# First experts' up products in three half-precision products, and the second attention's turned maxima one slot later

## The reference, cut to what matters

```
# layer 0, mixture of 8 experts (2048 tokens, capacity 256 each)
logits = xt @ Wg;  probs = softmax(logits)
sel    = top 256 tokens of each expert by probs     # which token goes where
out    = sum_e gate[:, e] * (gelu(xt @ W1[e]) @ W2[e])   # W1[e] 128x256, W2[e] 256x128
# layer 1, cross attention: 16 heads of 64, keys of valid length only
scores = rope(q) @ rope(k).T / 8, masked;  attn = softmax(scores);  out = attn @ v
```

## Time and profile before

| | |
|---|---|
| median of 3 runs | 2943.0 us (2940.43 to 2944.17) |
| the profiled execution | 2939.36 us |
| its span | 2937.2 us |
| TensorE busy | 2638.0 us (90%) |
| VectorE busy | 2006.5 us (68%) |
| ScalarE busy | 1450.8 us (49%) |
| GpSimd busy | 1374.3 us (47%) |
| first experts | 862 to 993.4 us of the span |
| second attention, its iterations | about 1047 to 2690 us |

### The profile page before, as it was taken

One profiled execution on the slowest core, in us unless ns is written; L12 is line 12 of the kernel. 1 busy time (PEld: TensorE's weight loads), 2 busy tenths in 40 slices (PEclk: granted clock), 3 DMA queues, 4 the chain that ended last, 5 costly groups with the idle time before them and its releaser, 6 DMA issues. The chain is left out here.

```text
span 2937.2 us, 82056 instructions
## 1 busy us (share of the span) xinstructions
PE 2638.0 (90%) x32600; PEld 1569.0 (53%) x32600; DVE 2006.5 (68%) x6348; ACT 1450.8 (49%) x2243; POOL 1374.3 (47%) x1221
## 2 busy tenths in 40 slices
PE   3679999999989569999999999999999999996598
PEld 2423333333355536666666666666666666664365
DVE  3468888888856567667766766766667667662655
ACT  2247777777744035546446455455464454443222
POOL 2000000000000038877878878878778788785100
PEclk8789999999989779999999999999999999998799
DMA  5421111111010110000000000000000000001000
GB/s 156 144 89 24 24 27 22 25 22 25 21 30 1 64 37 7 19 13 7 18 13 7 17 13 7 26 5 19 13 8 18 13 7 7 7 2 51 0 0 15
DMA packets 109630, 75.20 MB, mean 26 GB/s; under 512 B 43907, under 2 KB 101579, under 8 KB 108752
## 3 DMA queue, kind: packets, MB, share of 16 engines
q1 hardware_dynamic: 109264, 70.08, 8.5%
HBM read 56.61 MB, written 13.43 MB: 24 GB/s over the span
## 5 line engine op out<-in xcount | busy, mean ns | idle before, releaser
L1485 ACT ACTIVATE a_probs<-psS 128x1024 f32<-128x1024 f32 (+1 forms) x448 | 431.7, 964 | 630.0 <-PE psS L1366 625.9
L645 ACT ACTIVATE a_probs<-psS 128x1024 f32<-128x1024 f32 (+2 forms) x512 | 443.5, 866 | 207.0 <-PE psS L586 206.6
L1802 POOL TENSOR_TENSOR a_acc<-a_acc,a_probs 128x512 f32<-128x512 f32 x320 | 407.3, 1273 | 225.1 <-ACT a_probs L1485 221.9
L1389 PE MATMUL psX<-a_probs,a_values 128*64 128x256 f32 x3328 | 445.6, 385 | 1.6
L672 DVE CUSTOM_DVE_ANT_0 a_junk<-psT,a_mask 128x384 f16<-128x384 f32 (+1 forms) x683 | 378.2, 573 | 61.3 <-PE psT L562 41.6
L1804 POOL TENSOR_TENSOR a_acc<-a_acc,a_probs 128x512 f32<-128x512 f32 x320 | 407.1, 1272 | 25.1
L1646 DVE CUSTOM_DVE_ANT_0 a_junk<-psT,a_mask 128x400 f16<-128x400 f32 (+1 forms) x514 | 282.6, 573 | 153.8 <-PE psS L1341 86.3
L1646 DVE CUSTOM_DVE_ANT_0 a_junk<-psS,a_mask 128x400 f16<-128x400 f32 (+1 forms) x510 | 280.7, 573 | 150.9 <-PE psT L1341 88.3
L974 POOL MEMSET r_ones<- 128x128 f16 x1 | 0.2, 205 | 694.4 <-POOLq L719 694.4
L1389 PEld LDWEIGHTS psX<-a_probs,a_values 128*64 128x64 f32 x3328 | 224.1, 137 | 105.2 <-issue 24.6
L1776 POOL TENSOR_TENSOR a_klo<-a_kt,a_khi 128x400 f16<-128x400 f32 (+1 forms) x256 | 242.7, 948 | 18.6 <-ACT a_khi L1537 18.6
(11 more groups left out here) (332 smaller groups left out, 5561.4 us busy)
## 6 DMA issues: line engine op xcount, KB each, us to landing
a_kd<-p_kst SPq DMA_DIRECT2D x24, 416.0 KB, 3.4
a_wq<-in_wq SPq DMA_DIRECT2D x64, 128.0 KB, 2.1
a_keys<-a_kd SPq DMA_DIRECT2D x96, 75.0 KB
p_ctx<-in_ctx SPq DMA_DIRECT2D x8, 768.0 KB
a_ctx<-in_ctx SPq DMA_DIRECT2D x8, 768.0 KB
a_queries<-a_lowest SPq DMA_DIRECT2D x256, 0.5 KB, 2.0
p_mask_raw<-in_mask_t SPq DMA_DIRECT2D x16, 224.0 KB, 4.4
a_queries<-a_qd SPq DMA_DIRECT2D x64, 52.0 KB
```

The source lines that it names most:

```text
L645: nc.scalar.activation(dst, src, ACT.Exp).then_inc(exp_done, 1)
L1389: ins = nc.tensor.matmul(w.sums[n % 2][64 * hd:64 * hd + 64, 0:T], w.values[:, n % 2, c, 64 * hd:64 * hd + 64], w.probs[:, k % RING1, 2 * ...
L1485: nc.scalar.activation(dst, src, ACT.Exp).then_inc(exp_done, 1)
L1802: nc.gpsimd.tensor_tensor(acc, acc, src[:, :, 0, :], ALU.add).then_inc(sum_step, 1)
```

## The change

In the first experts the up product becomes three half-precision products of 512 columns: high part of the weights by high part of x, low by high, high by low. The weights are first multiplied by 64 on GpSimd, in place; ScalarE casts them to the high part, GpSimd subtracts for the low part; the Gelu divides by 64. The parts of x are made in the same way, quarter by quarter. `w1` is loaded into a part of `hid` that the last expert's Gelu writes later. In ScalarE's list the cast of the weights stands ahead of the copies of x. The counting products stand after half 4, 8, ..., 60, the last count after the first down unit, the ranks after the second. In the second attention `turn_max` and ScalarE's copy of it move from slot 1 to slot 2, behind that slot's values.

```
-FIRST_COUNT, COUNT_EVERY = 3, 3
+FIRST_COUNT, COUNT_EVERY = 4, 4
...
+        w1 = hid[:, X0 - 1, 0, :].rearrange("p (e f) -> p e f", e=X0)
+        w1_hi, w1_lo = sb("e0_w1_hi", [P, X0, F0], F16), sb("e0_w1_lo", [P, X0, F0], F16)
+        x_hi, x_lo = sb("e0_x_hi", [P, TOK], F16), sb("e0_x_lo", [P, TOK], F16)
...
+                    if e == 0 and h == 0:
+                        pe.wait_ge(x_split, blk + 1)
+                        if n < 2:
+                            pe.wait_ge(x_high, 2 * n + 2)
                     o = (2 * (n % 2) + h) * BANK
-                    ins = nc.tensor.matmul(m.psS[:, o:o + BANK], w1[:, e, h * P:(h + 1) * P],
-                                           m.xT[:, blk * BANK:(blk + 1) * BANK], start=True, stop=True)
+                    for i, (weights, moving) in enumerate(((w1_hi, x_hi), (w1_lo, x_hi), (w1_hi, x_lo))):
+                        ins = nc.tensor.matmul(m.psS[:, o:o + BANK], weights[:, e, h * P:(h + 1) * P],
+                                               moving[:, blk * BANK:(blk + 1) * BANK], start=(i == 0), stop=(i == 2))
...
-                pe.wait_ge(loaded, 32)
+                pe.wait_ge(w1_split, 1)
                 for half in range(2 * UNITS0):
                     up(half // 2, half % 2)
                     if half + 1 in count_after:
                         add_counts(count_after[half + 1])
-                    if half + 1 == GT_AFTER:
-                        add_counts(ROUNDS0)
-                    if half + 1 == RANK_AFTER:
-                        find_ranks()
+                pe.wait_ge(loaded, 16)
                 for n in range(UNITS0):
                     down(n)
+                    if n == 0:
+                        add_counts(ROUNDS0)
+                    if n == 1:
+                        find_ranks()
...
                 ln_scalar(nc, act, m, s, 1)
+                act.wait_ge(w1_scaled, 1)
+                nc.scalar.copy(w1_hi[:, :, :], w1).then_inc(w1_high, 1)
                 for q in range(3):
                     act.wait_ge(turned, q + 1)
                     nc.scalar.copy(m.xT[:, q * BANK:(q + 1) * BANK], m.psS[:, q * BANK:(q + 1) * BANK]).then_inc(xt_taken, 1)
+                    nc.scalar.copy(x_hi[:, q * BANK:(q + 1) * BANK], m.psS[:, q * BANK:(q + 1) * BANK]).then_inc(x_high, 1)
+                act.wait_ge(xt_last, 1)
+                nc.scalar.copy(x_hi[:, 3 * BANK:4 * BANK], m.psS[:, 3 * BANK:4 * BANK]).then_inc(x_high, 1)
...
+                pool.wait_ge(w1_loaded, 16)
+                nc.gpsimd.tensor_scalar(w1, w1, W1_SCALE, None, ALU.mult).then_inc(w1_scaled, 1)
+                pool.wait_ge(w1_high, 1)
+                nc.gpsimd.tensor_tensor(w1_lo[:, :, :], w1, w1_hi[:, :, :], ALU.subtract).then_inc(w1_split, 1)
+                for q in range(4):
+                    pool.wait_ge(x_high, q + 1)
+                    cols = slice(q * BANK, (q + 1) * BANK)
+                    nc.gpsimd.tensor_tensor(x_lo[:, cols], m.xT[:, cols], x_hi[:, cols], ALU.subtract).then_inc(x_split, 1)
...
-                    if is_pair(it + 1) and sl == 1:
+                    if is_pair(it + 1) and sl == 2:
                         turn_max(it + 1)
```

More of the change, by code:

```diff
@@ L837, in block_experts0 @@
     exp_done, counts, counted, steps, ready = (s.sem(f"e0_{n}") for n in ("exp", "counts", "counted", "steps", "ready"))
+    w1_scaled, w1_high, w1_split, x_high, x_split = (
+        s.sem(f"e0_{n}") for n in ("w1_scaled", "w1_high", "w1_split", "x_high", "x_split"))
+    w1_loaded = s.sem("e0_w1_loaded")
     loaded, wg_loaded, xt_last = s.sem("e0_loaded"), s.sem("e0_wg_loaded"), s.sem("e0_xt_last")
@@ L840, in block_experts0 @@
     count_after = {FIRST_COUNT + COUNT_EVERY * r: r for r in range(ROUNDS0)}
-    GT_AFTER = FIRST_COUNT + COUNT_EVERY * ROUNDS0 + 1
-    RANK_AFTER = GT_AFTER + 3
     PAD = 8
@@ L846, in sb @@
             return stack.enter_context(nc.sbuf_tensor(name, shape, dt))
-        w1, w2 = sb("w1", [P, X0, F0]), sb("w2", [P, X0, F0 // P, E])
+        w2 = sb("w2", [P, X0, F0 // P, E])
         hid = sb("e0_hid", [P, X0, 2, TOK])
+        w1 = hid[:, X0 - 1, 0, :].rearrange("p (e f) -> p e f", e=X0)
+        w1_hi, w1_lo = sb("e0_w1_hi", [P, X0, F0], F16), sb("e0_w1_lo", [P, X0, F0], F16)
+        x_hi, x_lo = sb("e0_x_hi", [P, TOK], F16), sb("e0_x_lo", [P, TOK], F16)
         wg = sb("wg", [P, X0])
@@ L878, in _ @@
                 sp.dma_start(wg[:, :], dram["wg"]).then_inc(wg_loaded, 16)
-                sp.dma_start(w1[:, :, :], dram["w1"].rearrange("e d f -> d e f")).then_inc(loaded, 16)
+                sp.dma_start(w1, dram["w1"].rearrange("e d f -> d e f")).then_inc(w1_loaded, 16)
                 sp.dma_start(w2[:, :, :, :], dram["w2"].rearrange("e (h f) d -> f e h d", f=P)).then_inc(loaded, 16)
@@ L969, in _ @@
                                          m.psS[:, o:o + 2 * BANK].rearrange("p (h t) -> p h t", h=2),
-                                         ACT.Gelu).then_inc(gelu_done, 1)
+                                         ACT.Gelu, scale=1.0 / W1_SCALE).then_inc(gelu_done, 1)
             @block.gpsimd
```

## The result

The changed kernel takes 2906.0 us (median of four executions, 2904.0 to 2907.5), the kernel before 2943.6 on the same chip: a ratio of 0.9873, interval 0.9856 to 0.989, 37.5 us less. Forecast were 2918.5 us and 24 us less, with a range that ended at 2908: the sign was right, the gain too small. The profiled execution took 2904.0 (a span of 2901.8), 35.4 less than the profiled one before.

What follows compares the result with a forecast made beforehand. TensorE's own order bounds the second attention, with 25.0 us of waits on the turned maxima; product and search are even in the first experts. Attention -20 and experts -4 give -24: 2918.5 us, range 2908 to 2932.

Steps and rivals of the forecast that it cites:

- the price of the new place: Second attention, slot 2: the four moved products cost 0.33 us from their start to the next weighing.
- the net: Second attention, ordinary iteration: slot 1's 0.76 us less slot 2's 0.33 gives 0.43 us, or 0.37, the wait alone.
- The bound of -25: Second attention, largest gain: 0.05 us more in 55 iterations and no loss in the seven normalising ones, -25 us.
- Slot 1: Second attention: without the maxima the weighing starts at 1804.42, not 1805.18; slot 1 loses 0.76 us.
- rivals 2 and 3: Second attention: the wait only moves, 2939 us, chance 0.08; or a late ScalarE copy makes it slower, 2966, chance 0.05.
- my lower bound: Second attention, smallest gain: iterations with VectorE's context statistics, and some ordinary ones, give their part back, -12 us.
- The normalising iterations: Second attention, seven iterations: slot 1 gains nothing, slot 2 pays 0.33 us; scores' wait grows from 1.3 to about 2.1.
- The load of the table: Normalising iterations: ScalarE loads a table ahead of slot 1's exponential, and the scores wait 1.34 us for it.
- The first experts: Stage of the up products: later start, faster products, ranks and last count moved behind; its end moves by -4.0 us.
- The round: First experts' token search, one count per four halves: 12 x 0.215 plus a count of 0.1, kept at 2.69 us.
- Rival 1: First experts give nothing: rounds take 3.0 us, +0.6 us; with an attention of -17, 2926 us; chance 0.17.
- A remark beside the sum: First experts: GpSimd's low parts would cost 1 us beyond 884.9 if a quarter of x took 1.3 us.

Runs made afterwards that it cites:

- experiment 2: Turned maxima's four products issued twice: in the changed kernel (slot 2) 2909.4 us, ratio 0.9895; in the kernel before (slot 1) 2943.5 us, ratio 1.0006.
- norm_later: Changed kernel with ScalarE's normalising of the next context begun one slot later, behind the exponential of slot 1: 2887.6 us, ratio 0.9821.
- before_twice: Kernel before with the four products of the turned maxima issued twice in slot 1: 2943.5 us against 2940.4, ratio 1.0006.
- one_pass: Changed kernel without GpSimd's weight scaling: ScalarE scales while casting, behind copies of x; VectorE makes the low part in one instruction: 2896.7 us, ratio 0.9852.

## Why the prediction was right in sign and short in size

**The step that failed** is the price of the new place: "In slot 2 the same four products come back, 0.33 us from their start to the next weighing". Measured: 0.08 from period to period, 0.11 for four more. The row was rightly read, but it was a row behind a stop, and its 0.33 us were three waiting instructions of the weighing, which go with the stop and don't come back (experiment 2). With 0.08 for 0.33 the net is 0.72 - 0.08 = 0.64, not 0.37 to 0.43, and over the 53 iterations 35 us, not 20. The bound of -25 failed with it (its own terms, 21.5 + 55 x 0.05, give 24.3): I had let the gain of a place range up to the idle time that the list of waits shows, and a stop costs more than its idle time.

**Slot 1** came out as worked (0.72 for 0.76), and that the wait would not return in slot 2 too: rivals 2 and 3 fall with the list of waits. **The statistics iterations** gave nothing back, against my lower bound: they won 0.74 to 0.84.

**The normalising iterations** went as said in kind (slot 1 gains nothing; the scores' wait grew to 2.21, forecast 2.1, wherever no slow stretch came before it), and paid 0.08 for 0.33. The load of the table, which I named as what stands ahead there, was not the cause of that wait: it stayed in norm_later, and the wait went. What no step contained is TensorE's lower clock: 4.7 us in three of them, behind the longer wait, and 1.7 in an iteration in which a batch leaves. Without these 6.4 us the miss would have been larger.

**The first experts** were sized within 1.3 us (-5.3 for -4.0). From the load's issue: router products at 13.95 us (forecast 14.2), ups at 22.3 (22.5), first count at 27.1 (27.6), downs at 66.6 (67.9). The round is the term that is most off, 2.62 for 2.69: 14 x 0.07 = 1.0. I had added 0.1 for the count to 12 x 0.215; the products alone are 0.213 apart, and the count fits into 0.06. Rival 1 (rounds of 3.0) falls. A remark beside the sum was wrong: four quarters of 1.3 us would end at 885.1, 0.2 us beyond 884.9 and not 1. By the time of the whole kernel the experts alone gave 2.7 us, and the interval there reaches from 0 to 5.3.

## What to carry to other kernels

Take the price of an instruction that is moved from a row in which its engine's queue runs: a gap from its start to the next instruction behind a stop can be waiting instructions of that next one, and leaves with the stop. Count a repeated short wait at idle time plus what then passes in the open (here 0.37 + 0.35), and count the waiting instructions behind it (here three of 0.106 us), which a timeline of the busy instructions doesn't show. And where a change lengthens one wait of TensorE, look at the granted clock behind it: the time lost there stands in no list of waits.

## What was not expected of the hardware

Behind a wait of 0.37 us TensorE took 0.33 us from the start of the maxima to the next weighing, with four products in between or eight, and 0.22 where one waiting instruction fewer stood there; that 0.22 was the same in the first iteration, at a granted clock of 0.50. In the changed kernel six of the seven normalising iterations have a stretch of 3.4 us at half the clock: three right behind the wait of 2.2 us, three some 5 us ahead of it, behind a wait of 1.9 us for VectorE that both kernels have; the seventh stretch lies behind a wait of 1.95 where a batch leaves. In the kernel before one such iteration has one. But in norm_later, where the wait of 2.2 us is gone, three stretches stayed, and before_twice, with the waits of the kernel before, has four; so what decides is left open. In one_pass VectorE's 16 normalising instructions, which read one table each, took 6.02 us for 4.19 while GpSimd made two quarters of x (2.46 us): the last two of them, begun beside GpSimd, took 1.25 each and not 0.34.
